# Expert weights: each second matrix split in its own expert's opening step, with three smaller moves

## The reference

```python
logits = xf @ w_router
probs = jax.nn.softmax(logits, axis=-1)
topk_w, topk_idx = jax.lax.top_k(probs, TOP_K)
...
h = jnp.einsum('te,ieh->tih', xf, w1) + b1
h = jax.nn.gelu(h)
out = jnp.einsum('tih,ihe->tie', h, w2) + b2
out = jnp.sum(out * weights[..., None], axis=1)
```

## Time and profile before

| What | Value |
|---|---|
| median of 3 runs | 2007.76 us (2006.26 to 2007.89) |
| the profiled execution | 2017.27 us, span 2015.1 us from first to last instruction |
| PE busy | 1829.8 us, 91% |
| DVE, ACT, POOL busy | 74%, 55%, 15% |
| the expert stage | about 511 to 969 us of the span |
| granted TensorE clock, mean | 0.955 |

### The profile page before, as it was taken

How to read it: one execution, slowest core, us unless ns; L and a number is a source line. 1 busy time by engine, 2 the same in 40 slices (tenths; PEclk the granted TensorE clock), 3 DMA queues, 4 the chain that set the end, 5 groups by cost and what they waited for, 6 DMA issues and landing times. The chain is left out here.

```text
span 2015.1 us, 31198 instructions
## 1 busy us (share of the span) xinstructions
PE 1829.8 (91%) x10840; PEld 1563.2 (78%) x10840; DVE 1489.5 (74%) x2966; ACT 1114.9 (55%) x1987; POOL 307.6 (15%) x282
## 2 busy tenths in 40 slices
PE   8999999996499999999677758999999999999999
PEld 5688888885499999999455536677788888888887
DVE  7567888886477666766599889998676776776675
ACT  4656666653344443443688857665456456456454
POOL 0001012233333323333100011111000000000000
PEclk9999999996699999999788889999999999999999
DMA  3199434413346545344434553333333143143141
GB/s 110 50 382 404 137 119 142 145 65 107 120 97 135 114 89 115 63 74 69 126 105 91 108 106 136 148 124 123 124 138 146 36 175 145 42 176 117 53 177 64
DMA packets 107986, 251.79 MB, mean 125 GB/s; under 512 B 8992, under 2 KB 51616, under 8 KB 99616
## 3 DMA queue, kind: packets, MB, share of 16 engines
q1 hardware_dynamic: 82288, 201.16, 28.3%
q0 software_dynamic: 23680, 46.28, 12.6%
q10 hardware_dynamic: 1888, 2.67, 0.4%
HBM read 172.88 MB, written 107.61 MB: 139 GB/s over the span
## 5 line engine op out<-in xcount | busy, mean ns | idle before, releaser
L1542 POOL DMA_INDIRECT tokens_behind_spare_rows<-yg,row_of_token x70 | 119.2, 1702 | 298.7 <-DVE row_of_token L1733 277.0
L1666 ACT ACTIVATE h<-bank,b1s 128x256 f32<-128x256 f32 x280 | 123.7, 472 | 36.3 <-PE bank L1470 21.1
L3175 ACT ACTIVATE hidden_quarter<-hidden_quarter,scl 128x512 f32<-128x512 f32 x96 | 67.6, 721 | 118.9 <-DVE hidden_quarter L3011 118.9
L1655 ACT ACTIVATE yg<-yt,own_gates 128x256 f32<-128x256 f32 x68 | 30.9, 502 | 184.0 <-DVE yt L1728 177.2
L1223 PE MATMUL bank<-st,L 128*128 128x128 f32 x768 | 117.2, 279 | 13.3 <-DVE st L573 13.2
L957 ACT ACTIVATE L<-bank 128x512 f32<-128x512 f32 x128 | 74.5, 594 | 95.7 <-PE bank L1215 84.7
L2384 PE MATMUL bank<-split_0h,hidden_weights 128*128 128x512 f32 x320 | 126.5, 395 | 0.0
L2384 PE MATMUL bank<-split_1h,hidden_weights 128*128 128x512 f32 x320 | 125.4, 392 | 0.1
L2385 PE MATMUL bank<-split_0l,hidden_weights 128*128 128x512 f32 x320 | 125.3, 391 | 0.0
L2385 PE MATMUL bank<-split_1l,hidden_weights 128*128 128x512 f32 x320 | 125.3, 391 | 0.0
L1215 PE MATMUL bank<-L 128*128 128x128 f32 x640 | 119.1, 276 | 1.2 <-ACT L L957 1.2
(11 more groups left out here) (485 smaller groups left out, 6028.1 us busy)
## 6 DMA issues: line engine op xcount, KB each, us to landing
hidden_weights<-hidden_weight_blocks SPq DMA_DIRECT2D x64, 1024.0 KB, 4.8
z_by_expert<-zero SPq DMA_DIRECT2D x64, 520.0 KB, 15.7
hidden_weight_blocks<-in_ffn_dram SPq DMA_DIRECT2D x14, 1024.0 KB
ckb<-in_ffn_dram POOLq DMA_DIRECT2D x32, 352.0 KB, 5.0
xg<-z_by_expert SPq DMA_DIRECT2D x36, 260.0 KB
x_tok<-in_w_dram SPq DMA_DIRECT2D x8, 1024.0 KB
x_tok<-x_T SPq DMA_DIRECT2D x16, 512.0 KB, 6.1
x_tok<-after_time_mix SPq DMA_DIRECT2D x15, 512.0 KB, 8.4
```

Source lines behind the costliest of these rows:

```text
L1542: pool.indirect_dma_start(x2_d, bass.IndirectOffsetOnAxis(to_row[:, j:j + 1].bitcast(u32), 0), yg[:, j, :], None, compute_op=ALU.add).then ...
L1666: nc.scalar.activation(h32[:, m, :], B[m % 4][:, 0:TT], ACT.Gelu_apprx_tanh, bias=b1s[:, e * KH + m:e * KH + m + 1]).then_inc(h_act, 1)
L3175: A_.activation(QB[to][:, m, :], src, ACT.Gelu, scale=scl[:, off[lay.name] + row:off[lay.name] + row + 1]).then_inc(g_act, 1)
```

## The change

Four moves, in 141 lines of diff.

1. The second matrix is split in its own expert's opening step. In the opening of e (1 to 7), ACT makes the high part of w2 of e right behind the Gelus, then that of w1 of e+1, with no wait for the down product. DVE makes the low part of w2 of e ahead of the fourth pair of h, and that of w1 of e+1 at the end. In expert 0 only w1 of expert 1 is left; expert 7 gets w2 of its own. w1 and w2 have semaphores of their own, and SP loads w2 of e+1, w1 of e+2 while expert e runs.
2. The bias addition `y` stands ahead of the low part.
3. The 67 semaphores are cleared by SP, behind its loop over the tiles and ahead of its last row load.
4. Of the three sums in the last opening step POOL makes two; the third comes behind the last scatter.

```diff
-            def weights(e):
-                if e >= 2:
-                    sp.wait_ge(ew_rdy, e - 1)
-                    sp.wait_ge(w2_rdy, e - 1)
+            def up_weights(e):
+                sp.wait_ge(ew_rdy, e - 1)
                 sp.dma_start(raw1[e % 2][:, :, :], w1_d[e]).then_inc(nw_ld[e % 2], 16)
-                sp.dma_start(raw2[e % 2][:, :, :], w2_d[e]).then_inc(nw_ld[e % 2], 16)
+
+            def down_weights(e):
+                sp.wait_ge(w2_rdy, e - 1)
+                sp.dma_start(raw2[e % 2][:, :, :], w2_d[e]).then_inc(nd_ld[e % 2], 16)
...
+                if 2 <= e < NE - 1:
+                    down_weights(e + 1)
                 if 1 <= e < NE - 2:
-                    weights(e + 2)
+                    up_weights(e + 2)
...
+            for done in first_sems:
+                sp.sem_clear(done)
             total = tile_count(sp)
...
                 if n == 6:
                     pool.wait_ge(hw_add, 16 * 13)
                     add(0, W_S4, 1, W_S2)
-                    for half in range(2):
-                        add(1, W_S4, half, W_S2)
+                    add(1, W_S4, 0, W_S2)
+                if n == 7:
+                    pool.wait_ge(hw_add, 16 * 13)
+                    add(1, W_S4, 1, W_S2)
...
+            hidden_sums(7)
...
             act.sem_inc(h_act, 4)
-            for done in first_sems:
-                act.sem_clear(done)
             act.wait_ge(ew_ld, 32)
...
+                if before < e and e >= 1:
+                    act.wait_ge(*down_landed(e))
+                    high_part(w2s, raw2, e)
                 if ahead:
                     act.wait_ge(*landed(e + 1))
                     high_part(w1s, raw1, e + 1)
-                    act.wait_ge(dn_ps, t * 2 + 2)
-                    high_part(w2s, raw2, e + 1)
...
                     else:
-                        if ahead:
-                            low_part(w1s, raw1, e + 1, 2 * e + 3, ew_rdy)
                         if not start:
                             y(before, t)
+                        if before < e and e >= 1:
+                            low_part(w2s, raw2, e, 2 * e + 2, w2_rdy)
                         dve.wait_ge(dn_ps, t * 2 + 2)
...
                 if ahead:
-                    low_part(w2s, raw2, e + 1, 2 * e + 4, w2_rdy)
+                    low_part(w1s, raw1, e + 1, 2 * e + 3, ew_rdy)
```

More of the change, by code:

```diff
@@ L262, in build @@
         ew_ld, v_ld = sem("expert_weights_loaded"), sem("vectors_loaded")
-        nw_ld = [sem(f"next_weights_loaded_{q}") for q in range(2)]
+        nw_ld = [sem(f"next_up_weights_loaded_{q}") for q in range(2)]
+        nd_ld = [sem(f"next_down_weights_loaded_{q}") for q in range(2)]
         x_rdy, lq_rdy, mk_cp = sem1("right_side_ready"), sem1("decayed_q_ready"), sem1("decay_rows_ready")
@@ L309, in _ @@
             sp.dma_start(free[:, KT * HID:KT * HID + HID // 128 * D].rearrange("p (k n) -> p k n", n=D),
-                         A["w2"].rearrange("e (k p) n -> e p k n", p=128)[1]).then_inc(nw_ld[1], 16)
+                         A["w2"].rearrange("e (k p) n -> e p k n", p=128)[1]).then_inc(nd_ld[1], 16)
             store_tokens(NB - 3)
@@ L1442, in landed, with down_landed @@
         def landed(e):
-            return nw_ld[e % 2], 32 * ((e + 1) // 2)
+            return nw_ld[e % 2], 16 * ((e + 1) // 2)
+        def down_landed(e):
+            return nd_ld[e % 2], 16 * ((e + 1) // 2)
         ptwo = ctx.enter_context(ExitStack())
@@ L1671, in step @@
                         act.dma_start(st1[:, :, :], w1_d[2]).then_inc(nw_ld[0], 16)
-                        act.dma_start(st2[:, :, :], w2_d[2]).then_inc(nw_ld[0], 16)
+                        act.dma_start(st2[:, :, :], w2_d[2]).then_inc(nd_ld[0], 16)
+                if before < e and e >= 1:
+                    act.wait_ge(*down_landed(e))
+                    high_part(w2s, raw2, e)
                 if ahead:
```

## The result

| | us |
|---|---|
| before, median (20 runs beside the change) | 2008.03 |
| after, median (20 runs) | 2004.36 |
| ratio, 95% interval | 0.9981 [0.9973, 0.9988] |
| profiled execution of after | 2001.18 (span 1999.4) |
| forecast | 1998.8 (1995.0 to 2003.5) |

The change gains 3.8 us (2.4 to 5.4) where 9.0 were forecast. The direction was right; the size was not, and the time lies above the range.

The account below looks back on a forecast made before the run. PE, busy for 91% of the span, was taken as the bound, so only its idle time could be won. Terms 7.6 + 1.0 + 1.9 - 1.5 = 9.0 us off 2007.76 gave 1998.8 us, range 1995.0 to 2003.5.

Parts of the forecast that it names:

- Openings of experts 1 to 6: Expert stage: all six PE waits of 1.34 us go, less 1.0 us for a late scatter behind opening 6; gain 7.0 us.
- Expert 0: First expert's opening step: DVE loses one low part and PE's 0.6 us wait goes.
- Opening of expert 7: One sum fewer ends POOL's multiplications earlier; PE's 3.16 us wait becomes 2.2, gain 1.0 us; w2's split costs 0.
- The clock: PE's fall to 1.2 GHz behind opening 7, costing 3.0 us, was assumed to remain.
- Rival A: PE's clock stays up behind opening 7: 3.0 us more gained, 1995.8 us; chance 0.20.
- Start of the stage: Expert stage start: with the clears off ACT, the first row split follows the transposes sooner; gain 1.9 us, range 0 to 1.9.
- rival B: The start gives nothing and the moved sum costs its upper bound: 1.9 + 2.2 us lost, 2002.9 us; chance 0.14.
- The seam: Start of the next stage: the last sum moves beside its loads; cost 1.5 us, bounds 0.3 and 3.7.
- Clears on SP: Between SP's last loop row load and the final one: 67 clears take 15.7 of 16.9 us; cost 0.
- landings of the scatter behind openings 1 to 5: Scatter lands in time for the gating; behind opening 1 it fits by 0.7 us and PE's 0.86 us slack.
- Rival C: Scatter lands late behind all openings, as behind the sixth: 5.0 us lost, 2003.8 us; chance 0.10.

Follow-up runs that it names:

- The sum alone: Kernel before with only the last weight sum moved behind the last scatter; ratio to before 1.0018 [1.0008, 1.0027], 3.6 us slower.
- the version with the sum back: Changed kernel with its third sum put back into expert 7's opening, nothing behind the last scatter; ratio to before 0.9962 [0.9948, 0.9976].

## Why the prediction was off

The traces add up to what was measured, if the start of the stage is left out. From the first transposes to the start of the last matmul of the down products, the stage takes 428.1 and 430.9 us in the two traces of before with the clears moved, and 421.9, 421.2 and 421.4 in three of after: 8.0 us less. The seam takes 3.5 us back on average (3.3, 3.9, 3.3). That leaves 4.5 us, where 3.8 (2.4 to 5.4) and, beside the experiments, 5.4 (3.2 to 7.6) were measured. Against the two traces of before itself, 433.7 and 429.2 us, it would be 10.0 - 3.5 = 6.5: they hold a late start, which the times of the clears' move do not bear out.

- **Openings of experts 1 to 6: the mechanism was right, the term too small.** 7.0 us were forecast; all six waits went. But a step with such a wait is 1.6 to 1.7 us longer than a plain one, not 1.34, which makes 6 x 1.66 = 10.0. The scatter behind the three sums of opening 6 came late, as worked out, and takes 0.9 to 1.5 us of it back (1.2 on average): 8.8. Expert 0, read at the sixth group of transposes, gave 1.3 (55.2 us from the first group in the two traces of before with the clears moved, 53.9 on average in three of after) where 0.6 was said.
- **Opening of expert 7: the step that failed.** It was +1.0 in the sum. By the distance between the groups of transposes, PE loses in four traces of the old order 3.5, 3.4, 5.9 and 5.9 us there (4.7 on average), and in three of the new one 6.6, 6.3 and 7.1 (6.7): -2.0, an error of 3.0. Two links were wrong.
  - That the low and the high part of w2 "are covered: cost 0". The prediction set the low part behind a yt "over 2 us behind POOL's end", which in before is the one at 929.88, and took DVE's idle time from 932 to 938. That is one step too late. In after the low part stands in the opening step, at 893.95, and POOL's sums start at 900.99. It does fit into DVE's idle time, but the row numbers stand behind it and POOL's work behind them. With one sum less, the multiplications still end 8.16 us behind the transposes instead of 6.90; with three sums 8.98. By the waits the low part costs PE 1.0 to 1.1 us (4.70 against 3.71 and 3.56); the times can't resolve that.
  - "The multiplications end that much earlier", so the wait shrinks by 1.0. The sum alone does bring the end 0.85 us forward, and PE's waits are 3.44 us instead of 3.15, because the hold falls on an earlier instruction. In the new order a sum less buys 0.1 to 0.4.
- **The clock.** "I leave the drop in the sum" took one trace for the rule. The same wait of 3.15 us had the fall in two traces of four; behind 4.7 us it fell in three of three. The fall was worth 2.4 us to the next transposes (5.9 against 3.5 lost), where 3.0 was said for it. The sum had it as certain before and after; before, half of the traces don't have it. Rival A asked whether the change would end a fall that in half of the traces was not there.
- **Start of the stage: 1.9 us forecast, none measured.** The profile does show the first up-product 1.3, 1.7 and 1.9 us later in three traces with slow clears on ACT. In time the clears' move is worth nothing in two comparisons, on chips where it isn't known whether ACT was slow. The lower bound of 0 was in the text, and this was half of rival B.
- **The seam: 1.5 forecast, 3.3 to 3.9 measured.** The bounds were 0.3 and 3.7, and the choice between them went by idle engine time in the first 2.5 us. The measured price is that of a sum that stands wholly ahead of the loads, in one trace a little above it. This was the other half of rival B.
- **Clears on SP, weight loads, landings of the scatter behind openings 1 to 5:** no cost, as forecast. PE never waited for rows in the last step, and no wait appeared in experts 1 to 5.

In one sum: 9.0 + 1.8 (openings) + 0.7 (expert 0) - 3.0 (opening 7) - 1.9 (start) - 2.0 (seam) = 4.6 us. Rival B named two of the three losses. Rival C's time, 2003.8, is the nearest, but its late scatters behind experts 1 to 5 did not come, so that is luck. No rival had a wait behind opening 7 that grows.

## What to carry to other kernels

Work of GpSimd on SBUF beside a busy VectorE has no price of its own: the two multiplications cost the matmuls nothing, waits of 3.7 us apiece or 6.8 us together, by whether VectorE had idle time at that spot. So look in VectorE's row for the gap that recurs in each step and put such work there. Work that fits into an engine's idle time is free only if nothing that others wait for stands behind it: the low part fitted, and the row numbers behind it came 2.1 us late. A transfer that "may as well go last" stands ahead of the next stage's first loads; where that stage starts with loads, as here, it can cost 3.2 to 3.9 us. And before a term of a sum rests on one stretch of one profile, above all a clock that fell once, take the step's length from group to group of a recurring instruction rather than the idle time in brackets.

## What the runs showed of the hardware

- A DVE instruction with its inputs in SBUF that is caught by GpSimd's work is held to the end of it, however small: a copy of 128x8 elements took 5.44 us (0.17 elsewhere), a cast of 128x512 6.39 (0.42). With three sums ahead, the version with the sum back split the hold in two:

```profile
900.04 1.83 DVE L1769 CAST hsh<-h 128x512 fp32r<-128x512 f32 x1
901.91 5.62 DVE L1771 TENSOR_TENSOR hsl<-h,hsh 128x512 fp32r<-128x512 f32 x1
```

```profile
900.12 3.18 POOL L1561 DMA_DIRECT2D hidden_weight_blocks<-hidden_weight_blocks  x3
902.01 4.96 POOL L1544 TENSOR_TENSOR x_tok<-x_tok 128x768 f32<-128x768 f32 x2
```

  The subtraction of two SBUF inputs is held by the multiplications too, and the cast ahead of it already while the sums are issued, before the first multiplication starts. What reads a PSUM bank was not held: in before the cast and the subtraction of the rows (921.34 to 922.74) took their usual 0.68 and 0.69 us while the profile has the first multiplication under way from 921.63. The Trainium skill (SBUF — State Buffer, Who interferes with whom) states that a DVE instruction with two SBUF inputs contends with a GpSimd one that reads SBUF; this row agrees, with 5.62 us where 0.69 is usual.
- It goes the other way as well: beside DVE's low part of 2.28 us GpSimd's scatter takes 3.02 us to issue instead of 1.54. A multiplication of 1.84 us took 3.40 where it met DVE's subtraction and cast; which of the two held it isn't shown.
- A PE wait of 1.34 us lengthened its step by 1.6 to 1.7 us.
- 67 semaphore clears on ACT took 15.7, 16.6, 16.2 and 4.5 us in four profiles. On two other chips their move to SP changed no time (over 0.8 and over 1.6 us of gain are excluded).
- A DMA of 512 KB that adds into memory, issued just ahead of the next stage, put off that stage's first matmul by 3.2 to 3.9 us. SP's issue of the second weight load took 1.03 us instead of 0.47 in the first trace, and 0.47 to 1.30 in the others with this order.
